# The residual sum one network stage earlier on VectorE, and the second norm's rows ahead of the next u on ScalarE

## The reference

```python
h = _layernorm(x) * (1 + ca) + sa
x = x + ga * _L0_attn_ref(h, ...)          # the "residual sum" of this document
h = _layernorm(x) * (1 + cb) + sb          # the "second norm"
x = x + gb * _L0_ffn_ref(h, ...)
# inside the attention:
freq_avg, phase_avg = freq.mean(-1), phase.mean(-1)       # from x @ wave_w.T
pos = clip(base + s_idx * freq_avg + phase_avg, 0, L - 1)
g = g_lo + frac * (g_hi - g_lo)                           # linear interpolation
out_h = einsum('blshd,blhs->blhd', g, w)                  # w = silu(x @ kernel_w.T + kernel_b)
return silu(out @ out_w.T)
# inside the experts:
mask = one_hot(top_k(softmax(logits)), E).sum(-2)
out = einsum('bse,ehd,bsd->bsh', mask, expert_w, h) + einsum('bse,eh->bsh', mask, expert_b)
```

## Time and profile before

| | value |
|---|---|
| median of 3 runs | 326.8 us (326.21 to 327.01) |
| profiled execution | 327.7 us |
| its span | 325.9 us, 5078 instructions |
| busy: DVE | 286.1 us, 88% |
| busy: PE | 266.9 us, 82% |
| busy: ACT | 217.6 us, 67% |
| busy: POOL | 44.0 us, 13% |
| mean granted TensorE clock | 0.895 of full speed |

### The profile page before, as it was taken

One profiled execution on the slowest core, in us unless ns is written; L12 is line 12 of the kernel. 1 busy time (PEld: TensorE's weight loads), 2 busy tenths in 40 slices (PEclk: granted clock), 3 DMA queues, 4 the chain that ended last, 5 costly groups with the idle time before them and its releaser, 6 DMA issues.

```text
span 325.9 us, 5078 instructions
## 1 busy us (share of the span) xinstructions
PE 266.9 (82%) x1720; PEld 185.7 (57%) x1720; DVE 286.1 (88%) x652; ACT 217.6 (67%) x539; POOL 44.0 (13%) x64
## 2 busy tenths in 40 slices
PE   6961982999499997999698969998897798986895
PEld 3531631864386476647574757657655575654674
DVE  8699998999979999999999999999999999903433
ACT  2562777589748996895689667897688567485010
POOL 6110033020301110033003200201000200011000
PEclk9596767599859999999799987999999979998599
DMA  5630000020003000500022000400040005000101
GB/s 162 206 79 1 2 0 0 0 68 0 0 3 138 10 1 0 164 0 3 0 78 86 0 2 1 165 0 0 4 161 0 3 0 164 0 1 2 32 0 48
DMA packets 12159, 12.91 MB, mean 40 GB/s; under 512 B 1171, under 2 KB 11110, under 8 KB 11366
## 3 DMA queue, kind: packets, MB, share of 16 engines
q1 hardware_dynamic: 11684, 12.19, 12.0%
q10 hardware_dynamic: 450, 0.40, 0.5%
HBM read 10.45 MB, written 2.15 MB: 39 GB/s over the span
## 4 chain that ended last, share of the span: by engine, by line
DVE 48%; PE 23%; issue 16%; ACT 10%; POOL 2%; ACTq 0%; DVEq 0%; POOLq 0%
DVE T L707 14%; DVE AT L739 13%; PE pT L919 7%; DVE hm L800 4%; PE pE L1008 4%; ACT A L463 3%; PE pR L899 2%; PE pL L970 2%; ACT xn L368 1%; DVE prodN L719 1%; DVE x L758 1%; DVE topi L775 1%; DVE endw L727 1%; PE pY L933 1%; DVE st L632 1%
## 5 line engine op out<-in xcount | busy, mean ns | idle before, releaser
L463 ACT ACTIVATE A<-pT 128x512 f32<-128x512 f32 x128 | 71.2, 596 | 44.9 <-PE pT L919 44.7
L919 PE MATMUL pT<-first,AT 128*128 128x128 f32 x512 | 83.3, 316 | 18.2 <-DVE AT L749 10.6
L919 PEld LDWEIGHTS pT<-first,AT 128*128 128x128 f32 x512 | 66.0, 162 | 34.4 <-ACT A L463 17.2
L707 DVE COPY_PREDICATED T<-mask,T 128x672 f32<-128x672 int16 (+11 forms) x54 | 82.9, 1536 | 1.5 <-DVE prodF L719 0.5
L739 DVE TENSOR_TENSOR AT<-T,c 128x2064 f32<-128x2064 f32 x32 | 72.3, 2301 | 0.1
L1008 PE MATMUL pE<-hm,late 128*128 128x256 f32 x240 | 57.4, 394 | 0.0
L1008 PEld LDWEIGHTS pE<-hm,late 128*128 128x128 f32 x240 | 45.5, 195 | 7.8 <-issue 0.2
L314 POOL TENSOR_SCALAR ve<-sq 128x4 f32<-128x4 f32 (+1 forms) x18 | 5.7, 314 | 252.6 <-ACT xn L354 127.7
L933 PE MATMUL pY<-A,hs 128*32 128x256 f32 x512 | 30.9, 382 | 0.0
L368 ACT ACTIVATE xn<-x,nm,rs 128x128 f32<-128x128 f32 x64 | 26.4, 479 | 5.5 <-POOL nm L318 5.5
L800 DVE TENSOR_TENSOR hm<-mkb,h2T 128x2048 f32<-128x2048 bf16 x13 | 29.7, 2285 | 0.0
(11 more groups left out here) (129 smaller groups left out, 340.7 us busy)
## 6 DMA issues: line engine op xcount, KB each, us to landing
mkb<-mask_rows SPq DMA_DIRECT2D x6, 1024.0 KB, 5.2
x<-in_x SPq DMA_DIRECT2D x7, 256.0 KB, 6.1
out<-x SPq DMA_DIRECT2D x7, 256.0 KB, 3.9
late<-in_late SPq DMA_DIRECT2D x1, 592.0 KB, 4.0
mkb<-mask_rows SPq DMA_DIRECT2D x1, 512.0 KB, 3.5
x<-in_x SPq DMA_DIRECT2D x2, 128.0 KB, 3.6
wmod<-in_wmod ACTq DMA_DIRECT2D x1, 256.0 KB, 3.3
out<-x SPq DMA_DIRECT2D x2, 128.0 KB, 3.3
```

What stands on the lines that cost most here:

```text
L463: nc.scalar.activation(A[b][:, m, 2 * j:2 * j + 2, :].rearrange("p h l -> p (h l)"), pT[k % 2][:, :], ACT.Copy).then_inc(a_A, 1)
L707: nc.vector.copy_predicated(rows[:, :, :, j0:j1], spread(mask[:, k, 0:w, j0:j1], [P, w, H, j1 - j0], 2), rows[:, :, :, j0 + (1 << bit):j1 ...
L919: ins = nc.tensor.transpose(pT[k % 2][:, c0:c0 + P], AT[:, 2 * b + i, 2 * j + a, m * P:(m + 1) * P], ident)
```

## The change

Two lines move; nothing is added or removed.

```diff
@@ ScalarE, loop
                 run(i, 1, front_hs)
+                run(i, -1, norm2)
                 run(i, 1, front_u)
-                run(i, -1, norm2)
                 run(i, -1, back_h2T)
@@ VectorE, loop
                 run(i, -2, masked, 0)
+                run(i, -1, residual)
                 run(i, 0, network, range(4, 5))
-                run(i, -1, residual)
                 second(i, -2, masked, 1)
```

## The result

| | before | changed |
|---|---|---|
| median of 17 runs | 327.01 us (325.99 to 328.51) | 329.17 us (326.29 to 331.86) |
| ratio, 95% interval | | 1.0058 (1.0034 to 1.0082) |
| span of the profiled execution | 325.9 us | 330.1 us |

The account below looks back on a forecast made before the run. VectorE was taken to bound the kernel, nearly half of the chain and hardly waiting in the loop. Terms of 1.66 (iteration 2), 1.33 (iteration 3) and 0.5 us (iteration 6) gave 3.5 us, so 330.3 us, range 327.7 to 332.0.

Parts of the forecast that it names:

- What it could bring: Loop: an earlier `residual` brings `nm` no earlier in iteration 2; the earlier norm in iterations 4 to 7 costed at 0.
- Iteration 1, `h2T` 0.80 us later: ScalarE, iteration 1: `h2T`, behind norm rows, `u` and `uR`, starts at 57.18 instead of 56.38, 0.80 us later.
- Iteration 1, the late `t_g`: VectorE, iteration 1: the late `t_g` of unit 0 costs nothing, covered by the 1.37 us wait at L650.
- Iteration 2, VectorE 1.28 us late behind the sum: VectorE at `residual`, iteration 2: it waits for `t_g`, given at 78.95, and leaves 1.28 us late.
- `nm` held until the first product ends: POOL, iteration 2: VectorE's first L739 product shuts out `nm` until 87.28; without that rule the change would cost 1.6 us less.
- `h2T` 1.66, `grid` 2.30, `route` 1.66 us late: Iteration 2 behind `nm`: `h2T` 1.66 us late, `grid` 2.30 us late waiting for `uR`, `route` 1.66 us late waiting for logits.
- Iteration 3, 1.33 us: VectorE, iteration 3: a new wait of 1.33 us for `t_g` at the new place of `residual`, nothing behind taking it back.
- Iteration 6, 0.5 us: VectorE, iteration 6: wait for `t_g` of 0 to 1.11 us depending on TensorE's clock; 0.5 taken as the middle.
- The end part: End part: PE gets the first `AT` of unit 7 about 3.5 us later than 260.30.
- rival (b): POOL, iteration 2: `nm` slips in ahead of the L739 pair, `h2T` some 0.1 us late; 328.9 us; chance 0.1.
- Rival (a): TensorE's clock, iteration 2: staying at 2.4 GHz, it makes `route` 0.8 us late instead of 1.66; 327.6 us; chance 0.2.
- Rival (c): Low clock at more places: `t_g` late in iteration 7 too, 1.7 us on top; 332.0 to 332.6 us; chance 0.12.

Follow-up runs that it names:

- the second run: The unaltered changed kernel measured once more against the kernel before: 329.41 us against 326.68 us, ratio 1.0039 (1.0006 to 1.0072).
- norm_from3: The kernel before, with the norm rows ahead of `u` on ScalarE only from iteration 3 on: 326.38 us against 326.60 us, ratio 0.9969.
- nm_first: Kernel before, norm rows ahead of `u` in iterations 1 and 2, VectorE waiting there for `nm` ahead of L739's products: 326.87 us against 326.76 us, ratio 0.9972.
- norm_only: The kernel before with only the norm rows moved ahead of `u` on ScalarE, the sum left in place: 329.21 us, ratio 1.0070 (1.0036 to 1.0103).
- upto2_warm: Kernel before, norm rows ahead of `u` in iterations 1 and 2, plus 9 and 6 extra matmuls in iteration 2: 329.20 us against 326.76 us, ratio 1.0035.

## Why the prediction held, and where it didn't

The forecast was 330.3 us in a range of 327.7 to 332.0, slower by more than 0.3%; measured were 329.17 us and a ratio of 1.0058. Step by step, 0.52 us taken off the changed trace:

- **What it could bring: nothing.** Right in both traces of the change, where `mu` stays directly behind the tanh values in iteration 2. With the sum alone moved, `nm` did slip in ahead of L739 in one trace and the wait at `route` went; over the executions that kernel wasn't faster. What the early sum brings from iteration 4 on wasn't tested alone.
- **Iteration 1, `h2T` 0.80 us later.** Measured 57.66 − 56.38 − 0.52 = 0.76 us.
- **Iteration 1, the late `t_g`: nothing.** Right in this trace: 0.87 us of waiting at L758, and the wait at L650 shrinks from 1.37 to 0.32 us. But that wait belongs to some executions only; the second run has none, and pays 0.60 us.
- **Iteration 2, VectorE 1.28 us late behind the sum.** In the first trace 79.36 − 77.67 − 0.52 = 1.17 us, with a wait of 0.91 us. In the second run of the change there was none: in that execution `t_g` came in time (76.24 + 0.66, L758 at 77.14). So this term changes from execution to execution.
- **`nm` held until the first product ends.** Right: from 85.85 to 87.88.
- **`h2T` 1.66, `grid` 2.30, `route` 1.66 us late.** Measured 1.74, 2.33 and 1.72 us.
- **Iteration 3, 1.33 us.** Over-sized: the wait was 0.63 us. VectorE is 120.73 − 117.74 − 0.52 = 2.47 us late at L650 behind it, 0.75 us more than at `route`. The distance from the start of the logits to that of the gate transposes was 113.68 − 92.20 = 21.48 us instead of 22.11 us. I had taken this chain as fixed.
- **Iteration 6, 0.5 us.** Nothing: no wait at L758, the same chain took 20.96 instead of 22.00 us, and its logits 1.06 instead of 1.40 us. Iteration 7, forecast 0: measured 0.23 us.
- **The end part.** PE got the first `AT` of unit 7 263.89 − 260.30 − 0.52 = 3.07 us late; the forecast had about 3.5. I let the rest follow VectorE unchanged. From VectorE's last L650 (257.11, before 253.81) to the end it took 0.9 us more, 0.62 us of it a wait of VectorE at L739 for ScalarE, and the granted clock from 262 to 270 was 0.57 where before it had been 0.81. Kernels that cost nothing have this wait too (0.56 us in `norm_from3`), so it isn't shown to come from the change.

```profile
281.99 2.31 DVE L739 TENSOR_TENSOR AT<-T,c 128x2064 f32<-128x2064 f32 x1 [0.62 <-ACT c L452]
```

So the sum of 3.5 us came out near for this execution (330.1 − 325.9 − 0.52 = 3.7 us, in part by other terms), but it is the slowest of the 17. Over all of them the cost is 2 us. The step that was mis-sized is the pair of iterations 3 and 6, 1.83 us forecast and 0.75 us found; the wait of iteration 2 was 0.91 us in one trace and none in the other. The sum was also built on one execution of the kernel before, and it describes the longest execution of the changed kernel; that the median of 329.17 lies in the range owes something to the range's width, since the forecast cost of 3.5 us is over one and a half times the measured one.

**What the parts showed beyond it.** I read the loss as mostly the early sum's (1.33 and 0.5 us are its waits). The runs give the sum alone about 1.1 us and the norm rows alone 2.5 us or more. I had seen how `nm` could slip past L739 when VectorE is late (rival (b)), but not the converse: without the early sum VectorE is earlier against POOL, and its pair of products catches `rs` too, so that `grid` waits 3.09 instead of 0.87 us. Rival (a), the clock, is a true condition of the part behind `uR`: raised by extra work it shortens the chain to `t_g` by 2.2 us, where I had put some 2. In the two traces of the change the low clock came as forecast; whether the executions at 326.3 to 326.6 us are rival (a) can't be said without their traces. Rival (c) had 1.7 us in iteration 7; the wait found there is 0.23 us.

The Trainium skill, "SBUF — State Buffer", section "Who interferes with whom", says that a VectorE instruction with two SBUF inputs contends with a GpSimd instruction that reads SBUF. The rows agree: in `nm_first`, where no product runs, `nm` takes 0.20 us and `rs` 1.03 us; in `norm_only`, where one does, 1.33 and 3.10 us.

## What to carry to other kernels

When an instruction is put ahead of another on an in-order engine, price it by the latest time at which its input can come, not by the time in one trace: here a chain of three small GpSimd instructions that began 0.08 us behind the start of a pair of VectorE products ended 5.58 us later (82.62 to 88.20), against 1.58 us when it ran free (82.26 to 83.84), and whoever was queued behind it paid the 4.0 us. Moving a wait earlier on the engine that sets the time can only help if somebody waits for the result; look for that wait first. And where a GpSimd result is urgent, letting VectorE wait for it ahead of a long two-input product can be cheaper than not waiting.

## What the hardware showed that I had not expected

- Each of POOL's small instructions is held anew. In `upto2_warm` `ve` took 2.26, `rs` 2.95 us, against 0.19 and 1.03 us in the free case; each ended only after the product of 2.3 us beside which it had started.
- The products of L739 aren't the only ones that hold POOL. In the kernel before `ve` took 1.84 us from 185.05, instead of 0.19, beside a `copy_predicated` of L707:

```profile
185.06 1.81 DVE L707 COPY_PREDICATED T<-mask,T 128x1376 f32<-128x1376 int16 x1
```

- Extra matmuls that compute nothing took the changed kernel's loss away (ratio 0.9960 instead of 1.0039 to 1.0058), with the granted clock from 87 to 96 at 1.00 instead of 0.50. The traces tie about 1.6 us of that to the clock (0.82, 0.55 and 0.22 us, above).
- The changed kernel's executions spread over 5.6 us. The mean clock goes with it only loosely: the three fastest had 0.900, the three slowest 0.881 to 0.897.
